# The closing layer norm of the last eight chunks, taken chunk by chunk behind the last sums

## The reference, cut to what matters

```python
def _layernorm(x, axis=-1, eps=1e-05):
    m = jnp.mean(x, axis=axis, keepdims=True)
    v = jnp.var(x, axis=axis, keepdims=True)
    return (x - m) / jnp.sqrt(v + eps)
...
x = L0_attn_x                              # (4, 512, 512) float32
x = _layernorm(x + _L0_attn_ref(...))
x = _layernorm(x + _L0_ffn_ref(...))
x = _layernorm(x + _L1_attn_ref(...))
x = _layernorm(x + _L1_ffn_ref(...))       # out = sum over experts of weight * (silu(gate) * up) @ Wd
```

## Time and profile before

| | us |
|---|---|
| median of three runs | 2333.25 |
| the profiled execution's own time | 2334.09 |
| its span, first to last instruction | 2332.4 |
| TensorE busy | 2268.7 (97%) |
| VectorE busy | 1573.5 (67%) |
| ScalarE busy | 880.1 (38%) |
| GpSimd busy | 761.1 (33%) |

### The profile page before, as it was taken

One profiled execution on the slowest core, in us unless ns is written; L12 is line 12 of the kernel. 1 busy time (PEld: TensorE's weight loads), 2 busy tenths in 40 slices (PEclk: granted clock), 3 DMA queues, 4 the chain that ended last, 5 costly groups with the idle time before them and its releaser, 6 DMA issues.

```text
span 2332.4 us, 30825 instructions
## 1 busy us (share of the span) xinstructions
PE 2268.7 (97%) x10746; PEld 1862.8 (80%) x10746; DVE 1573.5 (67%) x2385; ACT 880.1 (38%) x1436; POOL 761.1 (33%) x570
## 2 busy tenths in 40 slices
PE   8999999999999999999999899999999999999997
PEld 7887888888868888888877787778778778888885
DVE  5567777777778765683446666667677886666765
ACT  5456333333343222321222543324344444444441
POOL 0003544444413222341212532324234543333331
PEclk9999999999999999999999999999999999999999
DMA  6856222222250100000000211221011111111110
GB/s 214 227 157 176 64 73 72 75 73 72 59 204 1 37 19 19 23 1 19 1 1 28 82 55 55 81 90 74 28 55 55 55 67 51 54 54 54 54 36 36
DMA packets 92199, 154.36 MB, mean 66 GB/s; under 512 B 6320, under 2 KB 56496, under 8 KB 85824
## 3 DMA queue, kind: packets, MB, share of 16 engines
q1 hardware_dynamic: 92096, 153.02, 20.0%
HBM read 113.68 MB, written 39.32 MB: 66 GB/s over the span
## 4 chain that ended last, share of the span: by engine, by line
PE 62%; DVE 5%; issue 2%; ACT 1%; POOL 1%; POOLq 0%; DVEq 0%; ACTq 0%
PE attn_pvk L1235 4%; PE attn_pvk L1236 4%; PE attn_pvk L1237 4%; PE attn_pq L1235 2%; PE attn_pq L1236 2%; PE attn_pq L1237 2%; PE attn_po L1235 2%; PE attn_pv L1235 2%; PE attn_po L1236 2%; PE attn_po L1237 2%; PE attn_pv L1236 2%; PE attn_pv L1237 2%; PE attn_pv L85 2%; PE attn_pv L87 2%; PE attn_pv L86 2%
## 5 line engine op out<-in xcount | busy, mean ns | idle before, releaser
L2657 DVE TENSOR_TENSOR moe_a_lo<-moe_up_raw,moe_a_hi 128x512 fp32r<-128x512 f32 x192 | 183.1, 969 | 154.7 <-ACT moe_a_hi L2120 154.7
L2002 POOL TENSOR_TENSOR moe_h_lo<-moe_c_t,moe_h_hi 128x512 fp32r<-128x512 f32 x96 | 128.3, 1336 | 354.7 <-ACT moe_h_hi L2120 354.6
L1235 PE MATMUL attn_pvk<-moe_b_hi,moe_a_hi 128*128 128x512 f32 x512 | 201.7, 394 | 13.9 <-ACT moe_c_last L2246 6.0
L1237 PE MATMUL attn_pvk<-moe_b_hi,moe_a_lo 128*128 128x512 f32 x512 | 200.5, 392 | 0.0
L1236 PE MATMUL attn_pvk<-moe_b_lo,moe_a_hi 128*128 128x512 f32 x512 | 200.4, 391 | 0.0
L2120 ACT ACTIVATE moe_c_t<-attn_pvk 128x512 f32<-128x512 f32 x192 | 113.2, 596 | 186.7 <-PE attn_pvk L1237 184.7
L1349 POOL TENSOR_TENSOR ffn_h_lo<-ffn_h_f,ffn_h_hi 128x512 fp32r<-128x512 f32 x64 | 92.8, 1452 | 241.5 <-ACT ffn_h_hi L1416 241.5
L1593 DVE SCALAR_TENSOR_TENSOR all_acc<-attn_pvk,ffn_wts,all_acc 128x512 f32<-128x512 f32 x128 | 91.2, 749 | 93.2 <-PE attn_pvk L87 88.3
L2172 ACT ACTIVATE moe_c_t<-moe_c_t 128x512 f32<-128x512 f32 x96 | 60.4, 630 | 240.7 <-DVE moe_c_t L2729 240.7
L2120 ACT ACTIVATE moe_a_hi<-moe_up_raw 128x512 fp32r<-128x512 f32 x192 | 116.0, 625 | 56.4 <-POOL moe_up_raw L1972 56.4
L1235 PEld LDWEIGHTS attn_pvk<-moe_b_hi,moe_a_hi 128*128 128x128 f32 x512 | 96.7, 189 | 38.1 <-issue 11.3
(11 more groups left out here) (504 smaller groups left out, 6548.3 us busy)
## 6 DMA issues: line engine op xcount, KB each, us to landing
moe_up_raw<-in_e_up SPq DMA_DIRECT2D x28, 1024.0 KB, 5.7
moe_dn_raw<-in_e_dn SPq DMA_DIRECT2D x28, 512.0 KB, 3.7
xh<-mix_out_hi SPq DMA_DIRECT2D x32, 256.0 KB, 2.6
zs<-mix_out_z SPq DMA_DIRECT2D x32, 256.0 KB, 3.5
xl<-mix_out_lo SPq DMA_DIRECT2D x32, 256.0 KB, 3.9
mix_x<-xh SPq DMA_DIRECT2D x16, 512.0 KB, 4.1
mix_x<-xl SPq DMA_DIRECT2D x16, 512.0 KB, 5.3
mix_z_raw<-zs SPq DMA_DIRECT2D x16, 512.0 KB, 3.9
```

The source lines that it names most:

```text
L1235: pe.matmul(out, lh, rh, start=first, stop=False, skip_group_check=True)
L1237: return pe.matmul(out, ll, rh, start=False, stop=True, skip_group_check=True)
L2002: tt(h_lo[:, m, tok], src, raw(h_hi[:, m, tok]), ALU.subtract).then_inc(s_hlo, 1)
L2657: tt_(a_lo[q][:], src, raw(a_hi[q][:]), ALU.subtract).then_inc(s_alo, 1)
```

## The change

The last slot's sums are no longer closed in batches. Behind each sum VectorE computes the moments of the chunk before (`last_moments`, one `bn_aggr`) and then the chunk's own `bn_stats`, which waits for the chunk's sum through `s_free`. GpSimd makes scale and shift in five groups of columns (`GROUPS`: two, two, two, one, one), four instructions in each of the first four groups (EPS added, minus the mean, power, product) and two in the last. ScalarE normalizes chunks 8 to 14 in place by `Identity` with scale and bias from SBUF, and VectorE chunk 15 by one `tensor_scalar`. The stores stay on SyncE's queue in order; the last waits for its own semaphore. Three semaphores are new. The first half's closing norm keeps its instructions.

```diff
+        GROUPS = ((0, 2), (2, 4), (4, 6), (6, 7), (7, 8))
...
+        s_minus, s_moved, s_normed = k.sem("mean_turned"), k.sem("shift_ready"), k.sem("last_chunk_normalized")
...
             for ch in range(PC, NCH):
-                sp.wait_ge(s_norm, ch + 1)
+                if ch == NCH - 1:
+                    sp.wait_ge(s_normed, 1)
+                else:
+                    sp.wait_ge(s_norm, ch + 1)
                 sp.dma_start(t["out"][ch // CPB, bass.ts(ch % CPB, P)], acc[:, ch]).then_inc(s_out, 16)
...
+            def last_deviations(g):
+
+                a, b = GROUPS[g]
+                pool.wait_ge(s_mv, PC + b)
+                nc.gpsimd.tensor_scalar(rstd[:, a:b], mv[:, a:b, 1], EPS, None, ALU.add).then_inc(s_eps, 1)
+                if b < PC:
+                    nc.gpsimd.tensor_scalar(sum2[:, a:b], mv[:, a:b, 0], -1.0, None, ALU.mult).then_inc(s_minus, 1)
+                pool.wait_ge(s_eps, 2 + g)
+                nc.gpsimd.tensor_tensor(rstd[:, a:b], rstd[:, a:b], minus_half[:, 0:b - a], ALU.pow).then_inc(s_rstd, 1)
+                if b < PC:
+                    pool.wait_ge(s_minus, g + 1)
+                    pool.wait_ge(s_rstd, 2 + g)
+                    nc.gpsimd.tensor_tensor(sum2[:, a:b], sum2[:, a:b], rstd[:, a:b], ALU.mult).then_inc(s_moved, 1)
...
-            deviations(1)
+            for g in range(len(GROUPS)):
+                last_deviations(g)
...
             hidden_high(LAST, (0, 1), used_by(LAST, 7))
+            for g, (a, b) in enumerate(GROUPS[:-1]):
+                act.wait_ge(s_moved, g + 1)
+                for c in range(a, b):
+                    nc.scalar.activation(acc[:, PC + c], acc[:, PC + c], ACT.Identity, bias=sum2[:, c:c + 1],
+                                         scale=rstd[:, c:c + 1]).then_inc(s_norm, 1)
...
+            def last_moments(c):
+                dve.wait_ge(s_bn, PC + c + 1)
+                nc.vector.bn_aggr(mv[:, c], stats[:, c]).then_inc(s_mv, 1)
...
             for c in range(PC):
                 add_down(c, 1, NE - 1)
-                if c == CPB:
-                    finish(1, 0)
-            finish(1, 1)
-            for part in range(2, 7):
-                finish(1, part)
-            dve.wait_ge(s_norm, NCH)
+                if c:
+                    last_moments(c - 1)
+                dve.wait_ge(s_free, ring.base + c + 1)
+                nc.vector.bn_stats(stats[:, c], acc[:, PC + c]).then_inc(s_bn, 1)
+            last_moments(PC - 1)
+            dve.wait_ge(s_rstd, 1 + len(GROUPS))
+            ts(acc[:, NCH - 1], acc[:, NCH - 1], mv[:, PC - 1, 0:1], rstd[:, PC - 1:PC], ALU.subtract,
+               ALU.mult).then_inc(s_normed, 1)
+            dve.wait_ge(s_normed, 1)
```

More of the change, by code:

```diff
@@ L2002, in hidden_low, with deviations @@
                 tt(h_lo[:, m, tok], src, raw(h_hi[:, m, tok]), ALU.subtract).then_inc(s_hlo, 1)
-            def deviations(pair):
-                pool.wait_ge(s_mv, PC * pair + PC)
+            def deviations():
+                pool.wait_ge(s_mv, PC)
                 nc.gpsimd.tensor_scalar(rstd[:], mv[:, :, 1], EPS, None, ALU.add).then_inc(s_eps, 1)
-                pool.wait_ge(s_eps, pair + 1)
+                pool.wait_ge(s_eps, 1)
                 nc.gpsimd.tensor_tensor(rstd[:, 0:CPB], rstd[:, 0:CPB], minus_half[:], ALU.pow)
                 nc.gpsimd.tensor_tensor(rstd[:, CPB:PC], rstd[:, CPB:PC], minus_half[:], ALU.pow).then_inc(s_rstd, 1)
+            def last_deviations(g):
[10 more added lines that the diff above has]
+                    nc.gpsimd.tensor_tensor(sum2[:, a:b], sum2[:, a:b], rstd[:, a:b], ALU.mult).then_inc(s_moved, 1)
             def slot(n, u, s):
@@ L2021, in slot @@
                 if at(n, SLOTS + 1):
-                    deviations(0)
+                    deviations()
                 hidden_low(n, (0, 0))
@@ L2789, in router, with finish @@
                                  over(sum1[:], size), ALU.mult))
-            def finish(pair, part):
-                if part == 0 and not pair:
+            def finish(part):
+                if part == 0:
                     dve.wait_ge(s_free, ring_of(SLOTS + 1))
@@ L2796, in finish @@
                     for c in range(CPB * part, CPB * part + CPB):
-                        if pair:
-                            reach(dve, s_free, ring.base + c + 1)
-                        nc.vector.bn_stats(stats[:, c], acc[:, PC * pair + c]).then_inc(s_bn, 1)
+                        nc.vector.bn_stats(stats[:, c], acc[:, c]).then_inc(s_bn, 1)
                 if part == 2:
                     for c in range(PC):
-                        dve.wait_ge(s_bn, PC * pair + c + 1)
+                        dve.wait_ge(s_bn, c + 1)
                         nc.vector.bn_aggr(mv[:, c], stats[:, c]).then_inc(s_mv, 1)
                 if part == 3:
-                    dve.wait_ge(s_rstd, pair + 1)
+                    dve.wait_ge(s_rstd, 1)
                 if part >= 3:
                     for c in range(2 * (part - 3), 2 * (part - 3) + 2):
-                        ch = PC * pair + c
-                        ts(acc[:, ch], acc[:, ch], mv[:, c, 0:1], rstd[:, c:c + 1], ALU.subtract,
+                        ts(acc[:, c], acc[:, c], mv[:, c, 0:1], rstd[:, c:c + 1], ALU.subtract,
                            ALU.mult).then_inc(s_norm, 1)
+            def last_moments(c):
+                dve.wait_ge(s_bn, PC + c + 1)
+                nc.vector.bn_aggr(mv[:, c], stats[:, c]).then_inc(s_mv, 1)
             def side_work(n, c):
@@ L2819, in side_work @@
                 if at(n, SLOTS + 1) and c != 3:
-                    finish(0, c if c < 3 else c - 1)
+                    finish(c if c < 3 else c - 1)
             def last_product(n):
```

## The result

The changed kernel takes 2324.23 us (median of five runs, 2321.91 to 2327.16) against 2333.25 us (five runs, 2330.73 to 2336.75). The ratio is 0.9958, with a 95% interval from 0.9947 to 0.9969: faster by 0.42%, 7.2 to 12.4 us; the two medians lie 9.0 us apart. The forecast was 2324.4 us.

The account below looks back on a forecast made before the run. TensorE, busy 97%, was taken to bound the kernel up to the last down product; behind it, 1.17, 3.05, 4.28 and 0.4 us gained make 8.9, taking the median from 2333.25 to 2324.4 us, range 2321.0 to 2328.0.

Parts of the forecast that it names:

- The four gains of the sum: Last slot's end: sum 7 earlier 1.17, sum 7 to first VectorE norm 3.05, norm to last issue 4.28, landing 0.4.
- The ring: VectorE's sums, `bn_aggr` and stats per chunk: period 1.40 against TensorE's 1.36, no TensorE wait, sum 7 1.17 us earlier.
- The rival of a period of 1.65: VectorE's three instructions per chunk don't overlap, sum 7 starts at 2316.92, time 2326.1 us; chance 0.12.
- GpSimd is the new last wait: After the last moments at 2316.93, GpSimd's queue takes the last group at 2317.4, 0.5 late, ending it at 2318.22.
- The group's sum: GpSimd's group of two columns: 1.24 + 0.16 + 0.05 = 1.45 us.
- The stores: Last store issued at 2318.9, finds about 0.3 us of the one before, lands after 2.6 us (bounds 2.3, 3.0).
- One sign: In the changed profile's closing stores, DMA share not at its top for longer than 2 us.
- The norms: ScalarE's chunk 14 ready at 2318.47, VectorE's chunk 15 at 2318.81; of 3.74 us of eight norms, 0.55 stays.
- Rival, GpSimd held: VectorE's sums and stats hold two GpSimd instructions, last group 0.9 to 1.5 later, 2325.3 to 2325.9 us; chance 0.13.
- Rival, only the start moves: Stores of chunks 12 to 15 still queue on the DMA engines, landing 3.5, time 2326.7 us; chance 0.08.
- Rival, slower by issue time: Changed program text raises issue time in the 32 slots; 15.9 us more would give 2340.3 us; chance 0.03.

Follow-up runs that it names:

- the added powers: Changed kernel with three unused one-column powers on GpSimd: ahead of the last group, last landing 17.39 us against 15.84; ahead of the first, last norm 13.26 against 13.24.
- the two-input addition: Changed kernel plus two unused VectorE additions of two SBUF tiles each behind the last moments: span end 18.6 us behind the first sum, 18.2 expected without holding.
- early moments: Changed kernel with VectorE's new ring order kept, but one GpSimd batch and eight VectorE norms: ratio 0.9987 to the kernel before, last landing 21.70 us.
- early groups: Changed kernel with early moments and five GpSimd groups kept, but all eight norms on VectorE: ratio 0.9971 to the kernel before, last landing 19.07 us.
- groups and ScalarE without early moments: Changed kernel with stats in two batches of four and `bn_aggr` at the end: ratio 0.9996 to the kernel before, last landing 24.25 us.
- ScalarE with early moments but without early groups: Changed kernel with GpSimd making scale and shift in one batch behind the last moments: last landing 22.66 us, one execution.

## Why the prediction was right

The forecast named each time from the timeline before; shifted to the start of the first sum, it compares thus (us):

| | before | forecast | after |
|---|---|---|---|
| sum 7 starts | 10.97 | 9.80 | 9.67 |
| last moments ready | 14.63 | 11.56 | 11.35 |
| GpSimd takes the last group | 14.72 | 12.03 | 12.31 |
| last norm begun (before: first) | 17.11 | 12.89 | 13.24 |
| last store issued | 22.0 | 13.53 | 13.81 |
| last store landed | 25.05 | 16.13 | 15.84 |
| span ends | 27.03 | 18.13 | 18.20 |

The four gains of the sum, read from the same profiles: sum 7 earlier 1.30 (forecast 1.17); from sum 7 to the first norm on VectorE 2.57 (3.05); from there to the last issue 4.32 (4.28); landing 1.02 (0.4). Together 9.21 for 8.9.

- **The ring.** Right: TensorE's wait is gone and VectorE sets the pace with a period of 1.38 against the 1.40 taken and TensorE's 1.36. The rival of a period of 1.65 is out: `bn_aggr` did fit between the sum and its stats.
- **GpSimd is the new last wait.** Right, and shown by the added powers: in the last group they count in full, in the first not at all. Its size was too small: a group of two columns takes 1.63 (2314.30 to 2315.93) for 1.45, one of one column 1.48 for 1.24. The power of two columns was well placed, 0.71. The group's sum missed the step between a power's end and the product that waits for it, 0.14 to 0.15 us (2315.50 to 2315.65), and had too little between the starts of the two scalar instructions, 0.31 here. Together the last norm starts 0.35 late by the forecast.
- **The stores.** This is the term with the largest error. They landed in 2.0 us, not 2.6: seven tenths of a us apart they did not queue, and a store is quicker than the single row of before (2.3) showed. That row was not of a free store: it has an instruction packet among its data (last section). This is 0.57 too much in the forecast, and it covers the 0.35 above. The landing thus came 0.29 early, and barriers of 2.4 instead of 2.0 took that back, which brings the span's end to within 0.07. So the agreement at the end, and the one to 0.2 us in the median of runs that scatter by 5 us, are in part luck; what stands is that every step of the table is right to 0.35 us. One sign failed here: the DMA share was to be at its top for no longer than 2 us, and it stood at 0.94 for 2.25 us, since three stores in a row are only 0.7 to 0.8 us apart. The Trainium skill's estimate (SBUF — State Buffer, The DMA setup-cost knee) of 2.6 us for such a transfer was further off than the row.
- **The norms.** 0.55 on VectorE and 2.30 for ScalarE's last three (2.26 by the forecast's terms). No instruction stands ahead of ScalarE's first `Identity`.
- **Rival, GpSimd held.** It did not happen: GpSimd's small instructions take 0.22, 0.71 and 0.20 beside sums and stats. But its mechanism is real, as the two-input addition shows (0.46 us). Both agree with the rule of the Trainium skill (SBUF — State Buffer, Who interferes with whom) that excluded it here.
- **Rival, only the start moves.** It did not happen: the last stores are issued 0.7 us apart, SyncE's issues take 0.33 us, and the last six land 2.0 to 2.1 us behind their issue, none at 3.5.
- **Rival, slower by issue time.** No sign of it: the first sum of the last slot begins 0.27 us apart in the two profiles, and the medians differ by 9.0 us where the end alone accounts for 8.9. A shift ahead of the last slot by a us or two could hide in the scatter of the runs.

Where the gain came from is now in runs rather than in terms: early moments 3.35 us of landing, early groups 2.63 more, ScalarE 3.23 more, in that order. The three are single profiles each. Out of this order two cases were run: groups and ScalarE without early moments bring 0.80, and ScalarE with early moments but without early groups loses 0.96 against early moments alone.

## What to carry to other kernels

A closing stage that runs behind a paced loop is worth splitting from its first link on: here each further link split brought about 3 us, while links split behind one that was left in a batch brought 0.8 us or nothing. The first link left in a batch sets the time of all behind it. Once the links are fine, count the instructions per group on the slowest queue, since small instructions cost a fixed part each, and check what the last transfer finds in front of it before shaving tenths off the compute: here 0.3 us saved were nearly all given back to two stores that stood closer together.

## What the runs showed of the hardware that I had not expected

- GpSimd's instructions also took longer beside VectorE's `tensor_scalar` from SBUF to SBUF in float32, which has one tensor input: those of one column took 0.42 and 0.78 instead of 0.23 and 0.58, and a product of eight columns took 0.50, where one or two columns take 0.20 (no undisturbed one of eight columns is in the traces). No run was made to separate this. VectorE's sums out of PSUM and its stats, over 0.6 us each, did nothing of the kind. The rule of the Trainium skill (SBUF — State Buffer, Who interferes with whom) includes two-port modes of VectorE; that this `tensor_scalar` runs in one is only argued, from its 0.46 us for 512 elements where the stats need 0.61.
- A store of 256 KB landed 2.0 us behind its issue in most cases, 2.6 in others at the same spacing. What differs is in the traces: each of the ten profiles has a packet of 8 KB of the instruction queue (q14) while its first two stores move, 1.0 to 1.1 us behind the issue of the second. That second store then landed in 2.5 to 2.7 us, with 15 of its 16 parts at 2.0 to 2.1 and one late. The packet takes 0.31 to 0.50 us, and a few data packets around it take 0.12 to 0.20 us where most take 0.08. The kernel with powers ahead of the first group has a second such packet 1.1 us behind the issue of its last store, the one that took 2.6. Where stores follow each other at 0.7 us or closer, the late part stays late: in the burst of the kernel before the last store's fifteenth part landed at 2.5 and its last at 3.0. The coincidence holds in all ten profiles; no run moved the packet, so that it is the cause is argued.
- The spread between profiles lies almost wholly ahead of the last slot's sums: their first one starts between 2302.44 and 2307.58 in the ten profiles of kernels whose slots are alike, while from it to the last norm the kernel after and the one with powers ahead of the first group differ by 0.02 us.
